# Two graph layers on one core: masks dealt 1, 2, 1, 0, heads turned ahead of h1, second softmax drawn together, second output tile and second queries exchanged, heads 0 to 7 turned by DMA

## The reference

```python
h = relu(layernorm(x))
q, k, v = heads(h @ Wq + bq), heads(h @ Wk + bk), heads(h @ Wv + bv)   # 16 heads of 32
scores = where(adj == 0, -inf, q @ k.T / sqrt(32))
x = x + (softmax(scores, -1) @ v) @ Wo + bo
h = relu(layernorm(x))
alpha = maximum((h @ wq) @ (h @ wk).T, 0) * (adj != 0)
x = x + softmax(alpha, axis=1) @ (h @ weight)
```

## Time and profile before

| | |
|---|---|
| median of 3 runs | 1778.72 us |
| the profiled execution, its own time | 1777.45 us |
| its span, first to last instruction | 1775.7 us |
| TensorE busy | 1533.7 us, 86% of the span |
| VectorE busy | 1339.3 us, 75% |
| ScalarE busy | 1137.6 us, 64% |
| GpSimd busy | 948.0 us, 53% |
| mean granted TensorE clock | 0.978 |
| moved by DMA | 226.27 MB |

### The profile page before, as it was taken

The page is one execution under the profiler, slowest core; times in us unless marked ns, Lnnn a source line. Parts: engine busy times, 40 slices in busy tenths (PEclk is TensorE's granted clock), DMA queues, the critical chain, the costliest instruction groups (busy, mean ns, idle before and its releaser), DMA issues.

```text
span 1775.7 us, 50625 instructions
## 1 busy us (share of the span) xinstructions
PE 1533.7 (86%) x16561; PEld 1114.7 (63%) x16561; DVE 1339.3 (75%) x4234; ACT 1137.6 (64%) x2477; POOL 948.0 (53%) x1222
## 2 busy tenths in 40 slices
PE   2878989889888889888989898988898988988986
PEld 1556666666666666666666666666666666666663
DVE  6777777778777778778777778777878777877763
ACT  2666766666666666666666666666666666666661
POOL 0545555555545655555555555555555555554651
PEclk8999999999999999999999999999999999999999
DMA  6656655655655655655655655655555666465670
GB/s 213 126 100 134 125 121 133 139 129 121 134 130 120 139 136 113 141 125 113 142 136 120 140 122 114 143 133 133 123 124 126 133 137 137 111 137 129 108 125 30
DMA packets 656197, 226.27 MB, mean 127 GB/s; under 512 B 611488, under 2 KB 627872, under 8 KB 656160
## 3 DMA queue, kind: packets, MB, share of 16 engines
q1 hardware_dynamic: 636848, 188.57, 51.2%
q10 hardware_dynamic: 19312, 37.23, 6.8%
HBM read 57.94 MB, written 16.78 MB: 42 GB/s over the span
## 4 chain that ended last, share of the span: by engine, by line
PE 48%; DVE 29%; issue 10%; DMA 6%; ACT 3%; SPq 2%; POOL 1%; DVEq 1%; ACTq 0%; POOLq 0%
PE ring L405 39%; DVE wk_raw L844 7%; DMA turned<-wv_raw 6%; PE pv L476 3%; DVE xa L896 2%; DVE x L943 2%; SPq L364 2%; PE score L457 2%; DVE stage L922 2%; PE ring L537 2%; DVE stage L919 1%; DVE o_sum L859 1%; PE ring L511 1%; DVE work L896 1%; DVE half L901 1%
## 5 line engine op out<-in xcount | busy, mean ns | idle before, releaser
L1097 POOL TENSOR_TENSOR wv_raw<-wk_raw,wv_raw 128x512 f16<-128x512 f32 x512 | 607.2, 1187 | 641.9 <-ACT wv_raw L628 641.9
L615 ACT ACTIVATE wk_raw<-wk_raw,least 128x256 f32<-128x256 f32 x1024 | 459.0, 497 | 11.8 <-DVE least L844 11.7
L844 DVE CUSTOM_DVE_ANT_0 wk_raw<-score,far,undo_score 128x256 f32<-128x256 f32 x1024 | 448.8, 479 | 15.5 <-DVE far L1013 11.4
L628 ACT ACTIVATE wv_raw<-wk_raw 128x512 f16<-128x512 f32 x512 | 320.3, 626 | 9.7 <-issue 5.4
L476 PE MATMUL pv<-val,turned 128*128 128x65 f16 x2048 | 187.4, 193 | 39.7 <-DMA turned<-wv_raw 35.0
L1108 POOL TENSOR_TENSOR heads_out<-o_sum,o_rcp 128x64 f32<-128x64 f32 x512 | 139.2, 293 | 133.0 <-DVE o_sum L859 133.0
L476 PEld LDWEIGHTS pv<-val,turned 128*128 128x128 f16 x2048 | 152.3, 98 | 89.9 <-DMA turned<-wv_raw 44.9
L405 PE MATMUL ring<-wv_hi,h 128*128 128x256 f16 x1024 | 189.1, 273 | 0.0
L405 PE MATMUL ring<-h,wq_hi 128*128 128x256 f16 x1024 | 178.4, 276 | 7.8 <-DVE wk_lo L807 7.8
L478 PE MATMUL pv<-val,turned 128*128 128x33 f16 x2048 | 179.5, 180 | 0.0
L405 PE MATMUL ring<-h,wk_hi 128*128 128x256 f16 x1024 | 175.6, 273 | 0.0
(11 more groups left out here) (146 smaller groups left out, 3679.5 us busy)
## 6 DMA issues: line engine op xcount, KB each, us to landing
xin<-x_dram ACTq DMA_DIRECT2D x32, 512.0 KB, 3.8
out_dram<-xo SPq DMA_DIRECT2D x32, 512.0 KB, 3.4
xa<-x_dram ACTq DMA_DIRECT2D x31, 512.0 KB, 4.0
adj_in<-adj_dram SPq DMA_DIRECT2D x32, 256.0 KB, 2.8
turned<-wv_raw SPq DMA_TRANSPOSE x512, 3.1
adjt_in<-adj_t_dram SPq DMA_DIRECT2D x32, 256.0 KB, 3.1
wq_raw<-wq_dram SPq DMA_DIRECT2D x2, 512.0 KB, 6.7
wk_raw<-wk_dram SPq DMA_DIRECT2D x2, 512.0 KB, 8.4
```

Of the source, the lines that this page charges most:

```text
L615: last = nc.scalar.activation(probs[:, at, q, :], probs[:, at, q, :], ACT.Exp, bias=least[:, at, q:q + 1], scale=-1.0)
L628: nc.scalar.activation(halves[:, at, :, 0, :], probs[:, at, :, :], ACT.Copy).then_inc(hi["p"], 1)
L844: last = nc.vector.tensor_tensor_reduce(out=probs[:, at, q, :], in0=score[u % GROUP][:, q * NODES:(q + 1) * NODES], in1=far[:, q, :], scal ...
L1097: nc.gpsimd.tensor_tensor(halves[:, at, :, 1, :], probs[:, at, :, :], halves[:, at, :, 0, :], ALU.subtract).then_inc(lo["p"], 1)
```

## The change

Five edits of the order and three of where work is done:

1. Masks. `MASK_AHEAD = 4` becomes the table `MASKS_AHEAD`, by step modulo 4: one head, two heads, one head, none. All four heads of a group are masked within three steps of their scores. At step 5 the second of the two stands at the end of the step (`LATE_MASK`).
2. SyncE at step 6 issues the transpose of head 7 ahead of those of h1.
3. Second softmax. The maximum follows the masking of alpha at step 11; exponentials, reciprocal, high and low half all come at step 12, the exponentials of alpha ahead of those of the head.
4. hw1 moves from step 13 to 12 and qk1 from step 12 to 13.
5. Newton's step of the first norm moves from step 12 to 11, ahead of alpha's masking.
6. The normalisation of the first norm goes from VectorE to GpSimd (`first_normalise`), with a small VectorE instruction for the negative mean.
7. ot0 is gone: heads 0 to 7 are split while they still stand in `heads_out` (ScalarE `out_high`, VectorE `out_low`, step 11) and turned by two DMA transposes of 128x512 f16 at step 12 (`transpose_out`). wo0a, the first half of the projection, waits for these.
8. `oH` and `oL` become one tile `heads_t`; `norm_heads` waits for other semaphores accordingly.

```diff
-    ["alb", "ot0"],
+    ["alb"],
+    ["hw1"],
     ["qk1"],
-    ["hw1"],
...
-MASK_AHEAD, EXP_AHEAD, HALF_AHEAD, TURN_AHEAD = 4, 3, 2, 1
+MASKS_AHEAD = ((4,), (4, 5), (5,), ())
+EXP_AHEAD, HALF_AHEAD, TURN_AHEAD = 3, 2, 1
...
-STATS1, ROOT1, NORM1 = (8, 9), 10, 12
+STATS1, ROOT1, NORM1, LATE_MASK = (8, 9), 10, 11, 5
+OUT_STEP, TURN_OUT_STEP = 11, 12
...
+            def transpose_out(b):
+                sp.wait_ge(lo["o"], count(b, 1, 0))
...
+                for q in range(QT):
+                    sp.dma_start_transpose(
+                        heads_t[:, 0, :, :, q * P:(q + 1) * P].rearrange("p h d n -> p (h d) n"),
+                        half_out[:, q, :, :].rearrange("p h d -> p (h d)")).then_inc(out_in, 16)
...
-                    if s == TURN1_STEP and nxt:
-                        transpose_h1(n)
                     head = ahead(s, TURN_AHEAD, t, cur, nxt)
                     if head:
                         transpose_probs(*head)
+                    if s == TURN1_STEP and nxt:
+                        transpose_h1(n)
+                    if s == TURN_OUT_STEP and cur:
+                        transpose_out(t)
...
+            def out_high(b):
+                act.wait_ge(head_ok, count(b, HEADS // 2, HEADS // 4 - 1))
+                if started(b - 1):
+                    act.wait_ge(out_in, count(b - 1, QT, QT - 1) * 16)
+                nc.scalar.activation(half_out[:, :, 0, :], heads_out[:, :, 0:DIM // 2], ACT.Copy
+                                     ).then_inc(hi["o"], 1)
...
+                    if s == AL_STEP + 1 and prev:
+                        second_exponentials(p)
                     head = ahead(s, EXP_AHEAD, t, cur, nxt)
                     if head:
                         exponentials(*head)
-                    if prev:
-                        second_softmax(s, p)
+                    if s == AL_STEP + 1 and prev:
+                        second_high(p)
...
+                if which == 0:
+                    nc.vector.tensor_scalar(minus_mean[:], meanvar[0][:, :, 0], -1.0, None,
+                                            ALU.mult).then_inc(negated, 1)
...
+            def out_low(b):
+                dve.wait_ge(hi["o"], count(b, 1, 0))
+                nc.vector.tensor_tensor(half_out[:, :, 1, :], heads_out[:, :, 0:DIM // 2],
+                                        half_out[:, :, 0, :], ALU.subtract).then_inc(lo["o"], 1)
...
-                    head = ahead(s, MASK_AHEAD, t, cur, nxt)
-                    if head:
-                        mask(*head)
+                    for by in MASKS_AHEAD[s % GROUP][:1 if s == LATE_MASK else 2]:
+                        head = ahead(s, by, t, cur, nxt)
+                        if head:
+                            mask(*head)
...
                     if s == NORM1 and later:
                         reciprocal_deviation(0, n + 1)
-                        normalise(0, xa, xa, n + 1)
-                    if s == AL_STEP + 2 and prev:
+                    if s == AL_STEP + 1 and prev:
+                        second_reciprocal(p)
                         second_low(p)
...
+                    if s == OUT_STEP and cur:
+                        out_low(t)
+                    if s == LATE_MASK and cur:
+                        mask(s + 5, t)
...
+            def first_normalise(b):
+                pool.wait_ge(negated, count(b, 1, 0))
+                settle(pool, pool_settled)
+                for q in range(QT):
+                    nc.gpsimd.tensor_scalar(xa[:, q, :], xa[:, q, :], minus_mean[:, q:q + 1],
+                                            rstd[0][:, q:q + 1], ALU.add, ALU.mult
+                                            ).then_inc(normed[0], 1)
```

More of the change, by code:

```diff
@@ L65 @@
 BANK = {"qk2": 0, "wo0": 1, "ot1": 2, "wo1": 2, "qk3": 0, "v1": 1, "h2_0": 2, "h2_1": 0, "g0": 2,
-        "g1": 0, "hw0": 1, "qk0": 2, "al": 0, "ot0": 1, "qk1": 2, "hw1": 0, "v0": 1, "av0": 2,
+        "g1": 0, "hw0": 1, "qk0": 2, "al": 0, "qk1": 2, "hw1": 0, "v0": 1, "av0": 2,
         "av1": 0}
@@ L72 @@
         "hw0": -1, "g0": -1, "g1": -1, "hw1": -1, "qk0": 1, "al": -1,
-        "av0": -1, "av1": -1, "qk1": 1, "ot0": 0, "v0": 1}
+        "av0": -1, "av1": -1, "qk1": 1, "v0": 1}
 for name in ORDER:
@@ L218, in two_layers @@
         rstd = [sb(f"rstd{n}", [P, QT], f32) for n in (1, 2)]
+        minus_mean = sb("minus_mean", [P, QT], f32)
         eps = sb("eps", [P, 1], f32)
@@ L272, in two_layers @@
         RELEASE = {"v1": (lo["v"], 2, 1), "v0": (lo["v"], 2, 0),
-                   "ot0": (lo["ot"], 2, 0), "ot1": (lo["ot"], 2, 1),
+                   "ot1": (lo["ot"], 1, 0),
                    "wo0": (added, 2, 0), "wo1": (added, 2, 1),
@@ L541, in dense @@
                 elif name.startswith("wo"):
-                    pe.wait_ge(lo["ot"], count(b, 2, halves[-1]))
-                    signal(product(dst[:], lambda d: ((oH[:, d, tok], WH["wo"][:, d, :]),
-                                                      (oL[:, d, tok], WL["wo"][:, d, :])), KT,
-                                   halves), "wo")
+                    if 0 in halves:
+                        pe.wait_ge(out_in, count(b, QT, QT - 1) * 16)
+                    if 1 in halves:
+                        pe.wait_ge(lo["ot"], count(b, 1, 0))
+                    signal(product(dst[:], lambda d: ((heads_t[:, d // 2, 0, d % 2, tok], WH["wo"][:, d, :]),
+                                                      (heads_t[:, d // 2, 1, d % 2, tok], WL["wo"][:, d, :])),
+                                   KT, halves), "wo")
                 elif name.startswith("hw"):
@@ L692, in root, with second_exponentials, second_high @@
                                      bias=log_root[:, 0:1], scale=-0.5).then_inc(rooted[which], 1)
-            def second_softmax(s, b):
-                if s == AL_STEP + 1:
-                    act.wait_ge(l1_topped, count(b, 1, 0))
-                    for m in range(QT):
-                        last = nc.scalar.activation(work[:, 1, m * NODES:(m + 1) * NODES],
-                                                    work[:, 0, m * NODES:(m + 1) * NODES], ACT.Exp,
-                                                    bias=l1_max[:, m:m + 1], scale=undo[:, 5:6],
-                                                    accum_out=l1_sum[:, m:m + 1])
-                    last.then_inc(l1_exped, 1)
-                if s == AL_STEP + 2:
-                    act.wait_ge(l1_rcped, count(b, 1, 0))
-                    if started(b - 1):
-                        act.wait_ge(mm["av"], count(b - 1, 2, 1))
-                    for m in range(QT):
-                        last = nc.scalar.activation(eH[:, m, :], work[:, 1, m * NODES:(m + 1) * NODES],
-                                                    ACT.Copy, scale=l1_rcp[:, m:m + 1])
-                    last.then_inc(hi["e"], 1)
+            def second_exponentials(b):
+                act.wait_ge(l1_topped, count(b, 1, 0))
+                for m in range(QT):
+                    last = nc.scalar.activation(work[:, 1, m * NODES:(m + 1) * NODES],
+                                                work[:, 0, m * NODES:(m + 1) * NODES], ACT.Exp,
+                                                bias=l1_max[:, m:m + 1], scale=undo[:, 5:6],
+                                                accum_out=l1_sum[:, m:m + 1])
+                last.then_inc(l1_exped, 1)
+            def second_high(b):
+                act.wait_ge(l1_rcped, count(b, 1, 0))
+                if started(b - 1):
+                    act.wait_ge(mm["av"], count(b - 1, 2, 1))
+                for m in range(QT):
+                    last = nc.scalar.activation(eH[:, m, :], work[:, 1, m * NODES:(m + 1) * NODES],
+                                                ACT.Copy, scale=l1_rcp[:, m:m + 1])
+                last.then_inc(hi["e"], 1)
             def body(t, prev, cur, nxt, later):
@@ L754, in body @@
                         first_high(n + 1)
+                    if s == OUT_STEP and cur:
+                        out_high(t)
                     if s == XA_STEP and later:
@@ L1008, in body @@
                         aggregate(1, p)
-                    if s == HEADS - MASK_AHEAD and nxt:
+                    if s == HEADS - MASKS_AHEAD[0][0] and nxt:
                         dve.wait_ge(far_next_ok, count(n, 1, 0))
@@ L1123, in body @@
                         norm_heads(s // 2 - 1, t)
+                    if s == NORM1 and later:
+                        first_normalise(n + 1)
                     if s == X1_STEP and prev and not started(p - 1):
@@ L1151, in body @@
                         last.then_inc(far_next_ok, 1)
+            first_normalise(0)
             sweep(pool, body)
```

73 lines of the change are left out of this document (38 added, 35 removed).

## The result

| | before | changed | forecast |
|---|---|---|---|
| median of the runs, us | 1778.3 (4 runs) | 1681.1 (4 runs, 1679.6 to 1682.0) | 1637 |
| ratio to before | | 0.9449, 95% 0.9433 to 0.9465 | 0.920 |
| span of the profiled execution, us | 1775.7 | 1679.6 | |
| mean granted TensorE clock | 0.978 | 0.975 | |
| TensorE, VectorE, ScalarE, GpSimd busy, us | 1533.7, 1339.3, 1137.6, 948.0 | 1522.3, 1310.0, 1127.1, 1020.4 | |

A forecast was written before the change was run, and what follows sets the result against it. Chains between engines that release TensorE were taken as the bound. Terms of 4.15 us over 30 graphs (124.5), 19 for slow stretches and +2 at the start gave a span of 1634, so 1637 us; range 1595 to 1695.

The forecast's parts named there:

- Steps 2 to 6: Masks term: head 7's score wait goes and VectorE's chain to g0 is one mask shorter; 0.95 us a graph.
- steps 6 to 8: Masks and queue term: second score wait goes (0.85) and head 7's transpose wait (1.13); together 2.0 us a graph.
- Steps 11 to 14: Softmax, exchange, Newton and GpSimd term: chain from alpha's masking to av0 falls from 10.69 to 9.5 us; gain 1.2.
- Costed at nothing: Parts given no cost: GpSimd's normalisation, heads_out's DMA transposes in the queue, and out_high, replacing a high half of equal size.
- The stretches at half clock: After av0's wait: 12 slow stretches of 1.6 us counted as gone, 19 us, as the wait falls to 1.8 us.
- the wait at av0 stays long enough: Rival: chain short by 0.4 us, TensorE waits 2.2 us, stretches in every second graph; 1656 us; chance 0.17.
- stretches in all graphs: Worse form of the rival at av0: a slow stretch follows in every graph, given as 1675 us.
- half of the 124.5 us gone: Rival on masks: steps 2 to 6 only move their wait, av0's doesn't shrink; 1705 us; chance 0.08.
- The low half at 750.17: VectorE row taken as evidence against full exclusion: 0.77 us beside a GpSimd instruction, 0.67 without.
- The rival built on it: out_low waits for GpSimd's normalisation, av0's chain 0.6 to 2.4 us longer, stretches stay; 1674 to 1728 us; chance 0.17.
- The normalisation on GpSimd: Moved first normalisation: 2.5 to 4.3 us for both tiles, taken as 2.5; outside the chain to av0.
- The DMA turning: ot0's 0.5 us leaves TensorE's work between alpha and av0; heads_out's two transposes covered by eight steps to wo0a.

The follow-up runs named there:

- e5: Changed kernel with the mask table alone undone, one head masked in every step: 1704.0 us, ratio 0.9592.
- e4: Changed kernel with h1's transposes issued ahead of head 7's again at step 6: 1732.7 us, ratio 0.9739.
- e1: Changed kernel with Newton's step of the first norm and GpSimd's normalisation moved from step 11 to 10: 1629.9 us, ratio 0.9167.
- e9: Changed kernel with the negation of the mean ahead of Newton's first instruction instead of behind Newton's step: 1697.0 us, one run.
- e11: The e10 kernel with ot0 on TensorE again and no DMA turning of heads 0 to 7: 1595.7 us, ratio 0.8981.
- e6: Changed kernel with the exchange alone undone, qk1 at step 12 and hw1 at step 13: 1682.9 us, ratio 0.9474.
- e8: Changed kernel with ot0 on TensorE again at step 11 and no DMA transposes of heads 0 to 7: 1642.7 us, ratio 0.9252.
- e7: Changed kernel with the first normalisation back on VectorE, behind Newton's step at step 11: 1698.6 us, ratio 0.9566.
- e2: Changed kernel with head 2's mask at step 13 moved behind the second queries' low half: 1643.3 us, ratio 0.9247.
- e3: Changed kernel with the edits of e1 and e2 together: 1618.0 us, ratio 0.9096.
- e10: The e3 kernel with the second low half of h1 moved from step 4 to step 5, behind h2_1's: 1602.4 us, ratio 0.9013.
- e12: The e10 kernel unchanged, run again in the same rounds as e11: 1601.3 us, ratio 0.9006.

## Why the prediction was right and wrong

**What bounds the kernel** held: chains between engines, not busy time. VectorE's busy time fell by 29 us and TensorE's by 11, and the kernel by 97.

**Steps 2 to 6** gained 1.22 for 0.95, and **steps 6 to 8** 1.96 for 2.0. The mechanisms are shown: e5 brings the score waits back, e4 the transpose wait. What the forecast didn't say is that the two parts lean on each other (e4 loses 52 us, where the term for the transpose was 34).

**Steps 11 to 14** is where it failed, at the sentence that Newton's step "fills the time in which VectorE waited for alpha". Its instructions take 0.58 us and would have fitted; the first takes 0.94 by itself, because it begins inside a GpSimd instruction. That makes alpha's masking 0.36 late. The second failure is under "Costed at nothing": out_low was taken as no different from ot0's low half, but it reads SBUF twice, delays GpSimd by half a microsecond, and GpSimd then delays the copy of `far` by 0.56, which is what the 3.97 us are over the 3.4. Together 0.92 of the 0.94 that are missing. e1 removes both and gives 47.8 us a graph, where the forecast had 52.10 - 4.15 = 47.95.

**The stretches at half clock** followed from that. The forecast had 1.8 us of idle time ahead of av0 and named 0.4 us as its slack; the chain was short by more, and what came is the rival "the wait at av0 stays long enough", 2.2 us with a stretch in every second graph. Its 1656 lacks what the longer graphs cost. The 1.8 was also a slip of the sum: 9.5 us of chain less 8.0 of TensorE's work leave 1.5, and e1, whose chain is as forecast, has 1.55. Two sums among the rivals don't come out either: stretches in all graphs would add 30 x 1.6 to 1637, which is 1685 and not 1675, and with half of the 124.5 us gone it is 1699, or 1718 if the stretches stay too, and not 1705. Of the 44 us missed, 0.72 x 30 = 22 are the longer graphs and 14 x 1.63 = 23 the stretches that stayed.

**The rule that was weighed wrongly.** The low half at 750.17 was read as an overlap at a cost of 0.1 us. It began first, and it was GpSimd's pair beside it that took 2.74 us instead of 2.32: the reading looked at one side only. The rule of the Trainium skill (SBUF — State Buffer, Who interferes with whom), that such instructions exclude each other for a whole instruction and that the order of issue decides who waits, agrees with Newton's 0.94, with `far`'s 0.84, with out_low's 1.67 in e9 and with GpSimd's 1.66. The same section names copies and one-input tensor_scalar operations among those that can collide, which the held negation (0.95) and the copy bear out. The rival built on it had the wrong partner: the normalisation (741.82 to 743.34) was all but over as out_low began (743.27) and held up at most the scaling of the maximum ahead of it, 0.40 us against 0.23 in e11; the collisions that count were with the low halves.

**The normalisation on GpSimd** was mis-sized. Both ends of the bound, 2.5 and 4.3 us for two tiles, were too high; the trace of the changed kernel:

```profile
L1144 POOL TENSOR_SCALAR xa<-xa,minus_mean,rstd x64: 767/767/769, 7.7 to 1534.4; 128x512 f32<-128x512 f32 x64
```

0.77 us a tile, 1.52 for both. The earlier trace rows had two-tensor f32 (1.27) and int32 (1.07 for half the columns) and no form like it. It took nothing from the sum, but with 2.5 us the normalisation would have run 1 us into out_low.

**The exchange of hw1 and the queries** entered the sum as part of a new chain; e6 shows that it is worth nothing. **The DMA turning** was costed as 0.5 us less on TensorE; e8 and e11 show that it is worth nothing there and costs 38 us in the changed kernel.

## What to carry to other kernels

Before a VectorE instruction is moved, lay GpSimd's timeline beside its new place: one that works on 128x2 numbers can take a microsecond if it begins inside a GpSimd instruction, and when a pair seems to overlap, look at the length of both. Then an edit's worth depends on where TensorE's longest idle time lies: here the edits that brought it from 2.15 to 1.7 or less gave 23 us more than their own gain, and those that lost time elsewhere got most of as much back. Look at what follows every wait, and not only the longest. Undo the parts of a large change one at a time at the end; two of these were worth nothing or less.

## What the runs showed of the hardware

- VectorE's 128x2 f32 instructions, normally 0.15 to 0.17 us, took 0.94 (two inputs in SBUF) and 0.95 (one input) when they began 0.23 us into GpSimd's 1.15 us subtraction from SBUF. A 512-column bf16 copy took 0.84 instead of 0.28. A mask with its large input in PSUM, at 0.48, was not held. Newton's step beside GpSimd's int32 comparison took 0.16, and the comparison its usual length: not held either, though by the rule of the Trainium skill (SBUF — State Buffer, Who interferes with whom) it should be; why is open. That comparison is not free of collisions: the pair took 2.38 us instead of 2.10 where a one-input 128x512 f32 normalisation of VectorE ran at 1.08, and 2.10 where that took 1.39.
- In the other direction out_low, started 0.04 us ahead, made GpSimd's subtraction 1.66 us instead of 1.16; started 0.04 us behind, it took 1.67 itself.
- The half-clock stretch of 3.4 us came behind single idle times of TensorE of 1.7 to 2.5 us, and not behind each of them: in about every second graph at av0 before (2.24), in the changed kernel (2.19) and in e6 (2.50), in 20 of the 29 graphs of this length in e9 (2.07), in e4 at av0 or behind a wait for a transpose (2.09 at 753.65, 1.79 at 1009.25), and in e7 behind four waits for alpha's masking (1.73). Where the wait at av0 was 1.7 or less and no other was longer (e1, e2, e3, e5, e8, e10 to e12) it came nowhere in the loop. No length was found above which it always comes.
